# A graph network on one core: TensorE's attention order by pairs of quanta, a multiplication moved from GpSimd to VectorE, and counts read as 16-bit halves

## What is computed

```python
h = relu(layernorm(x)); h = (h @ W.T).reshape(n, 8, 32)
alpha = sum(h[src] * a_src) + sum(h[dst] * a_dst) + sum(relu(edge_attr @ edge_W.T + edge_b) * h[dst])
alpha = leaky(alpha, 0.2); ex = exp(alpha - segment_max(alpha, dst)[dst])
out = segment_sum(h[src] * ex / max(segment_sum(ex)[dst], 1e-10)) + bias
x = x + out                                  # attention
h = relu(layernorm(x))
h1 = relu(batch_norm(gcn_conv(h, W1, b1)))   # 256 -> 128
h2 = relu(batch_norm(gcn_conv(h1, W2, b2)))  # 128 -> 64
x = x + relu(concat(h, h1, h2) @ Wfc + bfc)
```

## Time and profile before

| what | value |
|---|---|
| median of 3 runs | 6951.39 us (6950.96 to 6955.41) |
| profiled execution: span | 6959.5 us |
| TensorE, matmuls | 4805.8 us busy (69%) |
| VectorE | 3523.0 us (51%) |
| ScalarE | 2073.8 us (30%) |
| GpSimd | 4908.5 us (71%) |
| mean granted TensorE clock | 0.693 |

### The profile page before, as it was taken

One profiled execution on the slowest core, in us unless ns is written; L12 is line 12 of the kernel. 1 busy time (PEld: TensorE's weight loads), 2 busy tenths in 40 slices (PEclk: granted clock), 3 DMA queues, 4 the chain that ended last, 5 costly groups with the idle time before them and its releaser, 6 DMA issues. The chain is left out here.

```text
span 6959.5 us, 113181 instructions
## 1 busy us (share of the span) xinstructions
PE 4805.8 (69%) x27409; PEld 3529.7 (51%) x27410; DVE 3523.0 (51%) x8745; ACT 2073.8 (30%) x5831; POOL 4908.5 (71%) x4806
## 2 busy tenths in 40 slices
PE   2699999999999994555555555556666666666655
PEld 1466666666666664344444444445544544444443
DVE  6688888888888888222222222223222222222224
ACT  3567777777777774000000000001000000000001
POOL 1777777776776756677777777774677777777775
PEclk9899999999999997555555555555555555555555
DMA  6777776777776655211111111111211111111115
GB/s 207 250 210 211 210 215 207 211 212 212 212 213 210 209 175 158 82 52 52 51 52 52 51 52 51 52 51 43 53 33 34 34 33 34 34 34 33 33 26 161
DMA packets 515795, 783.25 MB, mean 113 GB/s; under 512 B 143367, under 2 KB 392452, under 8 KB 514956
## 3 DMA queue, kind: packets, MB, share of 16 engines
q0 software_dynamic: 176176, 377.82, 21.0%
q1 hardware_dynamic: 303390, 369.82, 16.6%
q10 hardware_dynamic: 35758, 30.37, 1.4%
HBM read 695.07 MB, written 82.51 MB: 112 GB/s over the span
## 5 line engine op out<-in xcount | busy, mean ns | idle before, releaser
L1690 POOL DMA_INDIRECT c_g<-conv_table,c_idx x3128 | 3010.6, 962 | 1128.3 <-issue 952.9
L1767 PE MATMUL c_sums<-c_g,acc 128*128 x7040 | 1976.1, 441 | 1714.2 <-SPq L1653 1077.4
L1767 PEld LDWEIGHTS c_sums<-c_g,acc 128*128 128x128 f32 x7040 | 1626.4, 322 | 2220.1 <-issue 2210.1
L1002 POOL DMA_INDIRECT acc<-gat_table,ga_idx x1564 | 1615.8, 1033 | 653.0 <-issue 458.2
L1731 DVE TENSOR_TENSOR acc<-acc,c_sums 128x128 f32 (+1 forms) x1760 | 448.5, 255 | 2838.1 <-PE c_sums L1767 2821.7
L1386 PE MATMUL ga_sums<-ga_wg,ga_S 128*128 128x265 f32 x3520 | 999.3, 406 | 7.1 <-DVE ga_wg L1260 6.0
L1336 PE MATMUL ga_dstp<-ga_oht,ga_h 128*128 128x256 bf16 x5280 | 729.9, 275 | 76.0 <-DVE ga_prod L1181 69.7
L1386 PEld LDWEIGHTS ga_sums<-ga_wg,ga_S 128*128 128x128 f32 x3520 | 610.4, 193 | 171.4 <-issue 65.3
L1336 PEld LDWEIGHTS ga_dstp<-ga_oht,ga_h 128*128 128x128 bf16 x5280 | 505.7, 98 | 344.4 <-DVE ga_prod L1181 130.1
L1181 DVE SCALAR_TENSOR_TENSOR ga_prod<-acc,ga_a_dst,ga_dstp 128x512 f32<-128x512 f32 x880 | 645.0, 733 | 8.0 <-issue 6.7
L1077 ACT ACTIVATE ga_S<-iota_row,ga_dcol 128x128 f32<-128x128 f32 x1760 | 605.0, 392 | 73.5 <-issue 70.6
(11 more groups left out here) (253 smaller groups left out, 3731.5 us busy)
## 6 DMA issues: line engine op xcount, KB each, us to landing
ga_h<-h_parts SPq DMA_DIRECT2D x880, 192.0 KB
ga_dl<-dl_rows SPq DMA_DIRECT2D x110, 512.0 KB
c_g<-conv_table,c_idx POOLq DMA_INDIRECT x3128, 2.5
acc<-gat_table,ga_idx POOLq DMA_INDIRECT x1564
h_parts<-h_split SPq DMA_DIRECT2D x14, 1344.0 KB, 5.2
gat_table<-h_out SPq DMA_DIRECT2D x14, 952.0 KB
x_rows<-md_x SPq DMA_DIRECT2D x14, 896.0 KB, 7.1
fc_x<-x_rows ACTq DMA_DIRECT2D x98, 128.0 KB
```

The source lines that it names most:

```text
L1002: pool.indirect_dma_start(G[:, (v * PC + j) * HROW:(v * PC + j + 1) * HROW], None, gat_table, bass.IndirectOffsetOnAxis(idx[:, c:c + 1], 0 ...
L1690: pool.indirect_dma_start(G[:, c % (2 * SLOTS), :], None, table, bass.IndirectOffsetOnAxis(idx[:, c:c + 1], 0)).then_inc(rows_in[c // 2 % ...
L1767: last = nc.tensor.matmul(sums[:, b % R, 0:width], S[:, u * CH + 2 * b + j, :], flat[:, bass.ds(slots[b] * (2 * width) + j * width, width) ...
```

## The change

Three parts. In attention, TensorE's slot goes by two steps at a time: two adds, then the small products, then two quanta, then two dots; unit k - 2 and k - 1 are added at step k, so that units 6 and 7 are added at step 0 of the next slot. In the second dense stage VectorE does the multiplication by the inverse denominators (`share`), for group 0 ahead of the loop and for group g + 1 ahead of the add to x of group g; GpSimd adds the bias only; ScalarE makes the PSUM copies of six tiles of seven; rstd and shift of all groups are written straight into the arrays that stay, and the wait for the buffers that they had goes, in both dense stages. Last, lists of counts, and of free slots of the ring, are read into registers by the low 16-bit half of each 32-bit word.

```diff
+def low_halves(tab):
+    halves = tab.bitcast(U16)
+    return AP(halves.tensor, halves.offset, [list(halves.ap[0]), [2, tab.shape[-1]]])
...
-    rstd = [sb(ctx, f"{name}_rstd{u}", [P, GT]) for u in range(2)]
-    shift = [sb(ctx, f"{name}_shift{u}", [P, GT]) for u in range(2)]
+    if keep is None:
+        keep = [sb(ctx, f"{name}_{n}", [P, TILES]) for n in ("rstd", "shift")]
+    rstd, shift = ([t[:, g * GT:(g + 1) * GT] for g in range(GROUPS)] for t in keep)
...
-                u = g % 2
                 dve.wait_ge(s_sd, g + 1)
-                if g >= 2:
-                    dve.wait_ge(relu_done, GT * (g - 1))
-                link(nc.vector.reciprocal(rstd[u][:, :], sd[:, :]))
-                nc.vector.scalar_tensor_tensor(shift[u][:, :], mv[:, :, 0], -1.0, rstd[u][:, :], ALU.mult, ALU.mult).then_inc(s_norm, 1)
+                link(nc.vector.reciprocal(rstd[g], sd[:, :]))
+                nc.vector.scalar_tensor_tensor(shift[g], mv[:, :, 0], -1.0, rstd[g], ALU.mult, ALU.mult).then_inc(s_norm, 1)
                 dve.wait_ge(s_norm, g + 1)
-                if keep:
-                    nc.vector.tensor_copy(keep[0][:, g * GT:(g + 1) * GT], rstd[u][:, :])
-                    nc.vector.tensor_copy(keep[1][:, g * GT:(g + 1) * GT], shift[u][:, :])
...
-                            registers(row_tab[u][0:1, 1, :], mybir.EngineType.Activation, READY + 1, READY + 1 + UNITS // PB))
+                            registers(low_halves(row_tab[u][0:1, 1, :]), mybir.EngineType.Activation, READY + 1, READY + 1 + UNITS // PB))
...
                     t, m, v = x.at(), x.at(-1), x.odd(-1)
-                    for k in range(QS):
-                        if k == 0 and tail:
-                            add(x.at(-3), UL - 1)
-                        if k and c:
-                            add(x.at(-2), k - 1)
+                    for k in range(0, QS, 2):
+                        for n in (k - 2, k - 1):
+                            if k == 0 and tail:
+                                add(x.at(-3), UL + n)
+                            if k and c:
+                                add(x.at(-2), n)
                         if b and k == 2:
                             lines(m)
                         if b and k == 4:
                             carries(m, v)
-                        if a and k < QS - 2:
-                            quantum(t, k + 2)
-                        if more and k >= QS - 2:
-                            quantum(t + 1, k + 2 - QS)
-                        if a and k % 2:
-                            dot(t, k - 1)
-                            dot(t, k)
                         if b and k == 6:
                             factors(m)
                             turn_back(m)
+                        for q in (k + 2, k + 3):
+                            if a and q < QS:
+                                quantum(t, q)
+                            if more and q >= QS:
+                                quantum(t + 1, q - QS)
+                        if a:
+                            dot(t, k)
+                            dot(t, k + 1)
...
             nc.vector.tensor_scalar(dinv[:, :], acc[:, :, S0], 1.0, None, ALU.add).then_inc(deg_ready, 1)
+            dve.wait_ge(den_ready, 1)
+            share(dve, 0)
             link(nc.vector.tensor_scalar(dens(1, GROUPS), dens(1, GROUPS), 1e-10, None, ALU.max))
             nc.vector.reciprocal(dens(1, GROUPS), dens(1, GROUPS)).then_inc(den_ready, 1)
+            dve.wait_ge(den_ready, 2)
...
-                den = columns(g)[:, :, :, 0:1]
-                if g < 2:
-                    pool.wait_ge(den_ready, g + 1)
-                nc.gpsimd.tensor_tensor(heads, heads, spread(den, [[WROW, GT], [HCOLS, HEADS], [0, HDIM]]), ALU.mult).then_inc(scaled, 1)
                 pool.wait_ge(scaled, g + 1)
                 nc.gpsimd.tensor_tensor(heads, heads, spread(bias[:, :], [[0, GT], [HDIM, HEADS], [1, HDIM]]), ALU.add).then_inc(attended, 1)

+        def share(dve, g):
+            heads, den = columns(g)[:, :, :, 1:HCOLS], columns(g)[:, :, :, 0:1]
+            nc.vector.tensor_tensor(heads, heads, spread(den, [[WROW, GT], [HCOLS, HEADS], [0, HDIM]]), ALU.mult).then_inc(scaled, 1)
+
         def pre(dve, g, xg):
+            if g + 1 < GROUPS:
+                share(dve, g + 1)
             dve.wait_ge(attended, g + 1)
...
-                    lambda pe: pe.wait_ge(s_w, 32), pre=pre, keep=x1_norm, finish_act=finish_act, by_act=(1, 3, 5), hold=hold, at_end=at_end,
+                    lambda pe: pe.wait_ge(s_w, 32), pre=pre, keep=x1_norm, finish_act=finish_act, by_act=(0, 1, 2, 3, 4, 5), hold=hold, at_end=at_end,
```

More of the change, by code:

```diff
@@ L22 @@
 I32 = mybir.dt.int32
+U16 = mybir.dt.uint16
 ALU = mybir.AluOpType
@@ L575, in relu @@
                     act.wait_ge(turn_done, GT * (g - NH) + a + 1)
-                nc.scalar.activation(hn[g % NH][:, a, :], xg[g % NX][:, a, :], ACT.Relu, bias=shift[g % 2][:, a:a + 1],
-                                     scale=rstd[g % 2][:, a:a + 1]).then_inc(relu_done, 1)
+                nc.scalar.activation(hn[g % NH][:, a, :], xg[g % NX][:, a, :], ACT.Relu, bias=shift[g][:, a:a + 1],
+                                     scale=rstd[g][:, a:a + 1]).then_inc(relu_done, 1)
             def copy(n):
@@ L1602, in load_frees @@
     _, regs = nc.values_load_multi_w_load_instructions(
-        row, engines=[eng], min_val=USED, max_val=USED + UNITS,
+        low_halves(row), engines=[eng], min_val=USED, max_val=USED + UNITS,
         skip_runtime_bounds_check_because="unit numbers are clamped where they are worked out")
@@ L1758, in iteration @@
                     _, needs = nc.values_load_multi_w_load_instructions(
-                        need_row[0:1, bass.ds(m * UL, UL)], engines=[mybir.EngineType.PE], min_val=READY + 1, max_val=READY + 1 + UNITS,
+                        low_halves(need_row[0:1, bass.ds(m * UL, UL)]), engines=[mybir.EngineType.PE], min_val=READY + 1, max_val=READY + 1 + UNITS,
                         skip_runtime_bounds_check_because="pair numbers are clamped where they are worked out")
```

## The result

| | before | after |
|---|---|---|
| median | 6951.18 us | 7068.64 us (7064.67 to 7069.59, 4 runs) |
| ratio | | 1.0172, 95% interval 1.0158 to 1.0187 |
| profiled execution: span | 6959.5 us | 7062.3 us |
| attention, first to last TensorE instruction | 2299.2 us | 2458.0 us (+158.8) |
| second dense stage, first to last instruction | 177.0 us | 131.3 us (-45.7) |

The change costs 117 us; 99 were forecast. The stages were cut out of the trace by the first and last instruction of each, the convolutions by the starts of GpSimd's first and last gather. Attention is 159 us longer, 46 of them come back in the second dense stage; the convolutions, where GpSimd sets the pace, moved by 7 us in all.

A forecast was written before the change was run, and what follows sets the result against it. Attention was taken as set by waits between TensorE (96% busy) and VectorE (87%) within a slot, the convolutions by GpSimd's DMAs. -41 (dense) + 140 (pairs) + 0 (halves) = +99 us on 6951.39 gave 7050 us, range 6930 to 7110.

The forecast's parts named there:

- the likeliest case: Whole kernel: slower than before, 7050 us; chance 0.68.
- pairs of quanta: Attention, TensorE's order by two steps: two new stalls less shorter starts and attribute waits, +140 us.
- halves: Lists of counts and free slots read by 16-bit halves: loaded as before, eight numbers by one load, 0 us.
- second dense stage: VectorE takes over the product, GpSimd only adds the bias: groups 8.9 us apart, -41 us.
- The sums of pair 6: Attention: unit 6's add moves behind the close, VectorE's flush waits, TensorE stalls 0.80 us more a slot at quantum 3.
- The carries: Attention: unit 4's add no longer covers the chain from carries to quantum 7's six non-encoder matmuls: +0.90 us a slot.
- the absorption: Attention: a longer slot gives attribute loads more time, taking back 27 of TensorE's 31.9 us of encoder waits.
- the shorter starts: Attention: paired adds and paired quanta start sooner behind one another on TensorE, saving 0.18 us a slot.
- the variance step: Second dense stage, VectorE: finds GpSimd's bias add still running, costing 0 to 0.6 us a group, 0.5 taken.
- the wait for the square root: Second dense stage, VectorE behind ScalarE and TensorE: shrinks from 1.30 us a group to between 0 and 1.30, 0.5 taken.
- its rival: Second dense stage: GpSimd gets its port first, each add to x waits 3.5 us more, +4 us, 7095 us; chance 0.11.
- The rival that VectorE's idle places cover the new waits: Attention keeps only its savings, -52 us; whole kernel 6858 us, or up to 6930 if partly covered; chance 0.16.

The follow-up runs named there:

- whole-word pairs: The changed kernel with counts loaded as whole words again, each cut to its low 16 bits by a register operation: 7004.36 us, ratio 1.0061.

## Why the prediction was right, and where its terms were off

The direction, the range and the likeliest case held. The sum was 99 us, the measurement 117, but two terms were off by more than that, by -56 and +71, and nearly cancelled: that the sum came so near is luck.

| step | forecast | measured |
|---|---|---|
| pairs of quanta | +140 | +84 |
| halves | 0 | +71 (+47 in the old order) |
| second dense stage | -41 | -46 |
| sum | +99 | +109 by these terms, +103 by the two profiled spans, +117 by the medians |

**The sums of pair 6: right.** A new stall of 0.80 was forecast at S of Q3; it waits 0.73 here, and its start behind its E went from 0.22 to 1.10 us in the mean. The chain was forecast at 3.83 us and is 3.87. Moving the add back took 28 us with it, less than 110 x 0.80, because another wait of 0.54 comes in its place, that of the chain from the close, for which A6 was the cover.

**The carries: the mechanism right, the size off.** That "the stall is 1.51" rests on one slot, in which the chain from c to S of Q7 took 2.96 us. Over the slots of the kernel before it takes 2.61 in the median and 3.14 in the mean, after 2.61 and 2.63 (worked out, as all medians and means of slots here, from the starts in the slots between 500 and 2400 us). Two things were mixed in the row: a fixed chain of 2.6 us, and now and then a late list of targets ahead of product 5 (59.9 us of idle time before that one-hot, 19.4 with the pairs). In the kernel before the chain is more than 0.5 us above 2.61 in 30 of 92 slots, and in all 30 VectorE stood over 0.3 us before that one-hot; with whole-word pairs it is in 8 of 88. In the median S of Q7 starts 0.90 later behind its E than before (0.49 to 1.39), the 0.90 forecast; in the mean only 0.48 (1.02 to 1.50), since the longer slot does away with most of the late lists.

**The failed term is the absorption.** "I take back 27 of the 31.9 us" counted only what TensorE's encoder matmuls waited for the attributes. The slots of the kernel before take 20.62 us in the mean, with whole-word pairs 21.40. By starts, in us a slot: Q3 +0.88, Q7 +0.48, the attributes at Q4 (from l to its S) 0.66 to 0.39, -0.27, and the remainder -0.31: some 0.16 of it is the wait for attributes at Q0 of the next slot, which goes, and the rest is near the 0.18 forecast for the shorter starts. Together +0.78, x 110 = 85. The ledger without any absorption was +1.52, so 0.74 a slot, 82 us, was absorbed, three times what I took back: 0.42 by the late lists at Q7 and 0.43 by the attributes, against 0.08 more than forecast at Q3 and 0.03 less from the short starts. The place that I did not look at is the mean of S of Q7 against its median in the kernel before.

**Halves: wrong.** "If it doubled or removed ScalarE's stand without cover it would be 77 us either way" was the bound, and that the value came out near it is chance: the stand grew to 2.7 times, 129 us over the slots, and part of it was covered or came back. The step that failed is that the load by halves was priced as the one by words, and that ScalarE's 27% of idle time was taken as its cover. ScalarE's stand went from 0.67 to 1.84, 1.17 us, and it lies ahead of a one-hot that TensorE's in-order queue needs next: 0.75 us a slot at the add of unit 3 in the new order, 0.90 in the old one, where half of it comes back at later waits. An engine idle for a quarter of the time had no slack at this place. In the convolutions, where GpSimd's queue is the pace, the same slower loads cost nothing, as forecast.

**Second dense stage: right.** 8.56 us a group (8.9 forecast), from the first add to x to the last 2895.33 - 2783.47 = 111.9 us (before 156.35, forecast 114 for the same stretch); the variance step took 0.50 us in place of 0.17, 0.33 more where 0.5 was taken, and the wait for the square root shrank from 1.30 to 0.27, where 0.5 was taken. That VectorE's add gets SBUF ahead of GpSimd's, a choice that the prediction made, was worth 41 us: the other order leaves 4 us of gain (172.6 against 177.0 us) where its rival had 4 of loss.

The rival that VectorE's idle places cover the new waits is refuted by S's waits of 0.7 and 1.0 us in every slot between 500 and 2400 us. TensorE's share of attention fell to 88% (90 forecast). The attention of 2380 us under "What would show it" was the 2241 us stretch of the earlier trace rows plus 140; from first to last instruction attention took 2299 before, so the forecast stands for 2439, and 2458 was measured.

## What to carry to other kernels

Price a moved instruction by the chain that it leaves, over many slots: a stall's median shows the fixed chain, its mean the rare late loads, and a longer slot gives back only the second. Before a list is read in another width, time one load; it stands in an in-order queue, and what matters is what the next instruction in that queue feeds, not how idle the engine is. When a load is late, look first at when it was issued and what stood ahead of it in its queue, and only then at its buffer. When a part is judged by the whole, losses and gains hide each other: here the dense stage's gain, alone, is faster than before by 0.6%, and with the carries one add earlier by 1.0%.

## Not expected of the hardware

- A load of eight 16-bit numbers into registers takes 1.71 us on ScalarE and 1.93 on TensorE's queue, one of eight 32-bit numbers 0.55 and 0.59; sixteen contiguous 16-bit numbers take 3.37 and 3.80. On GpSimd eight take 1.82 or 1.83 us at either width.
- On another chip of the same kind the same kernel took 8661 us in place of 6951 to 6964, and which order of TensorE was best changed. Its transfer packets took the time that they took before (173 and 168 ns); SyncE's register instructions took 0.156 us in the mean in place of 0.035.
